# Six loops of a one-core transformer kernel written out as straight code, and a reordered state space layer

## The reference

```python
x = x + L0_xattn(layernorm(x), ctx, ctx, mask)   # 16 heads, softmax over 257 context rows
x = x + L0_attn(layernorm(x))                    # state space layer: s_t = A_t*s_(t-1) + Bx_t, 16 states per channel
x = x + L0_ffn(layernorm(x))                     # 256 -> 1024 -> 256 with quantized hidden values
x = x + L1_xattn(layernorm(x), ctx, ctx)         # 16 heads, sigmoid scores
x = x + L1_attn(layernorm(x))                    # self attention, softmax over 32 tokens
x = x + L1_ffn(layernorm(x))                     # 8 experts, each token goes to the likeliest
```

## Time and profile before

| | us |
|---|---|
| median of 3 runs | 3127.29 (3118.89 to 3130.5) |
| the profiled execution's own time | 3123.87 |
| its span, first to last instruction | 3122.1 |
| `softmax_attention` | 17 to 955 |
| `state_space` | 955 to 1470 |
| `quantized_ffn` | 1470 to 1624 |
| `sigmoid_attention` | 1624 to 2324 |
| `self_attention` | 2324 to 2667 |
| `sort_tokens`, `expert_tiles` | 2667 to 2805, to 3122 |

### The profile page before, as it was taken

How to read it: one execution, slowest core, us unless ns; L and a number is a source line. 1 busy time by engine, 2 the same in 40 slices (tenths; PEclk the granted TensorE clock), 3 DMA queues, 4 the chain that set the end, 5 groups by cost and what they waited for, 6 DMA issues and landing times. The chain is left out here.

```text
span 3122.1 us, 105389 instructions
## 1 busy us (share of the span) xinstructions
PE 2561.8 (82%) x38670; PEld 2034.0 (65%) x38671; DVE 2130.9 (68%) x4719; ACT 1878.5 (60%) x4388; POOL 1542.9 (49%) x1680
## 2 busy tenths in 40 slices
PE   3989889899893899996778989989967878509888
PEld 2867777677782577774446868768755666507666
DVE  5978878788794788886355757657665887643333
ACT  3867667677684788883346767667654665333333
POOL 4655656556562355552006656656635776052222
PEclk9999999999996899998898999999987998559999
DMA  4212212112110000000003212112100000641110
GB/s 144 67 59 59 64 51 64 58 51 64 57 30 14 1 1 1 0 1 14 16 14 91 66 50 62 59 52 61 59 18 3 2 2 2 206 159 34 33 34 27
DMA packets 120602, 144.45 MB, mean 46 GB/s; under 512 B 12912, under 2 KB 111632, under 8 KB 118064
## 3 DMA queue, kind: packets, MB, share of 16 engines
q1 hardware_dynamic: 115568, 124.40, 13.2%
q0 software_dynamic: 4672, 14.57, 1.3%
HBM read 123.71 MB, written 15.22 MB: 44 GB/s over the span
## 5 line engine op out<-in xcount | busy, mean ns | idle before, releaser
L1368 DVE SCALAR_TENSOR_TENSOR x_pTl<-x_psS,x_pTh 128x1024 f16<-128x1024 f32 x128 | 156.8, 1225 | 206.8 <-ACT x_pTh L1276 206.8
L2077 DVE TENSOR_TENSOR_SCAN m_s<-m_a,m_psBx 128x2048 f32<-128x2048 f32 x64 | 282.6, 4415 | 16.0 <-PE m_psBx L1852 15.6
L791 DVE CUSTOM_DVE_ANT_0 x_prob<-x_psS,x_masked,x_prob 128x256 f32<-128x256 f32 x512 | 216.6, 478 | 73.5 <-PE x_psS L548 71.7
L664 ACT ACTIVATE x_prob<-x_prob,x_low 128x257 f32<-128x257 f32 x512 | 253.5, 503 | 20.6 <-DVE x_low L791 20.6
L680 ACT ACTIVATE x_kh<-x_psK,x_bk 128x256 f16<-128x256 f32 x256 | 107.5, 471 | 238.9 <-PE x_psK L432 238.9
L1863 PE MATMUL m_psS<-m_s,all_ident 128*128 128x256 f32 x1024 | 237.3, 385 | 0.9 <-DVE m_s L2077 0.9
L1863 PEld LDWEIGHTS m_psS<-m_s,all_ident 128*128 128x128 f32 x1024 | 190.0, 190 | 46.3 <-issue 21.5
L1984 ACT ACTIVATE m_a<-m_dt,m_rate 128x248 f32<-128x248 f32 x512 | 205.6, 490 | 4.3 <-DVE m_s L2077 4.1
L2982 ACT ACTIVATE e1t_g<-e1t_psH,e1t_bias 128x128 f32<-128x128 f32 x312 | 89.2, 368 | 194.5 <-PE e1t_psH L2931 194.5
L1057 POOL TENSOR_TENSOR x_qbdh<-x_qh,all_mask4h 128x1024 f16<-128x1024 f16 x32 | 60.6, 1895 | 226.7 <-DVE x_ql L1349 226.7
L806 DVE SCALAR_TENSOR_TENSOR x_pTl<-x_psT,x_pTh 128x512 f16<-128x512 f32 x256 | 163.5, 679 | 4.9 <-ACT x_pTh L672 4.0
(11 more groups left out here) (558 smaller groups left out, 10542.0 us busy)
## 6 DMA issues: line engine op xcount, KB each, us to landing
x_ctx<-in_ctxT SPq DMA_DIRECT2D x64, 1024.0 KB, 5.7
x_mraw<-in_mask SPq DMA_DIRECT2D x128, 128.5 KB, 2.7
e1r_stage<-in_L_ffn_w SPq DMA_DIRECT2D x16, 1024.0 KB, 5.0
e_rows<-e1r_pad POOLq DMA_DIRECT2D x1, 5070.0 KB, 19.5
e1t_row<-e_rows SPq DMA_DIRECT2D x39, 130.0 KB, 2.1
all_xres<-in_x SPq DMA_DIRECT2D x1, 4096.0 KB, 14.8
x_vxr<-x_vx SPq DMA_DIRECT2D x128, 32.0 KB, 3.2
x_vxr<-x_vx SPq DMA_DIRECT2D x96, 8.0 KB, 2.0
```

What stands on the lines that cost most here:

```text
L664: act.activation(prob[c % 4][:, h, :], prob[c % 4][:, h, :], ACT.Exp, bias=low[c % 4][:, h:h + 1], scale=-1.0, accum_out=sm[c % 2][:, h:h ...
L791: dve.tensor_tensor_reduce(prob[c % 4][:, h, 0:LAST], psS[:, to:to + LAST], masked[gp][:, j, 0:LAST], -SC, prob[c % 4][:, h, LAST:S2], ALU ...
L1368: dve.scalar_tensor_tensor(pT[c % 4][1][:].rearrange("p r k n -> p (r k n)"), psS[c % 2][:], PS, pT[c % 4][0][:].rearrange("p r k n -> p ( ...
L2077: dve.tensor_tensor_scan(rows(S), rows(A), psBx[:], 0.0, ALU.mult, ALU.add).then_inc(scan_done, 1)
```

## The change

The loops of `softmax_attention`, `sigmoid_attention`, `quantized_ffn`, `state_space`, `self_attention` and `expert_tiles` become straight code on every engine. The loops of `sort_tokens` and of the layer norm's statistics stay. In `state_space` five pieces change places as well. The first hunk of `run` stands six times, at lines 249, 979, 1469, 1667, 2173 and 2878 of before; it is shown once.

```diff
@@ -249,10 +249,8 @@
         def run(eng, body):
-            body(0)
-            with eng.Fori(1, LASTI) as i:
+            for i in range(LASTI + 1):
                 body(i)
-            body(LASTI)
...
@@ -1754,10 +1746,9 @@
                 for c in range(U):
                     if exists(i, c, 1):
                         spread_b(*at(i, c, 1))
+                        dt_u(*at(i, c, 1))
                     if exists(i, c, -2):
                         residual(*at(i, c, -2))
-                    if exists(i, c, 1):
-                        dt_u(*at(i, c, 1))
@@ -1899,14 +1890,14 @@
                     drive(i, c, 2)
                     state_sum(i, c, 0, 0)
+                    if exists(i, c, 2):
+                        dbl(*at(i, c, 2))
                     if exists(i, c, -1):
                         out(*at(i, c, -1))
-                    if exists(i, c, 2):
-                        dbl(*at(i, c, 2))
                     drive(i, c, 3)
-                    state_sum(i, c, 0, 1)
                     if exists(i, c, 2):
                         dt_c(*at(i, c, 2))
+                    state_sum(i, c, 0, 1)
@@ -2000,10 +1991,10 @@
                 for c in range(U):
+                    if exists(i, c, 1):
+                        softplus_log(*at(i, c, 1))
                     decay(i, c, 1, 0)
                     decay(i, c, 1, 1)
-                    if exists(i, c, 1):
-                        softplus_log(*at(i, c, 1))
@@ -2114,9 +2105,9 @@
                     scan(i, c, 2)
                     if exists(i, c, 2):
                         lo_pb(*at(i, c, 2))
-                    scan(i, c, 3)
                     if exists(i, c, -1):
                         gate(*at(i, c, -1))
+                    scan(i, c, 3)
```

## The result

| | median us | runs |
|---|---|---|
| before | 3124.8 | 3118.89 to 3130.5 |
| after | 2881.9 | 2880.12 to 2884.12 |

A forecast was written before the change was run, and what follows sets the result against it. PE was taken as the bound, its gaps in softmax_attention being stalls at the backward branch. Gains of 98 + 45.5 + 25.5 + 4 + 32 = 205 us from 3123.9 gave 2919, predicted as 2920, range 2892 to 2968.

The forecast's parts named there:

- Each iteration becomes like the first, 49.8 us.: softmax_attention: without backward branches every iteration takes as long as the loop's first, which no stall precedes.
- the term of 98: softmax_attention: gain of 98 us from removing 13 backward branches, bounds 71 and 108.
- just this argument for `expert_tiles`: expert_tiles: tiles take 7.06 us straight, 7.64 in the loop, because register instructions stand ahead of matmuls that wait for nothing else.
- The stall itself: softmax_attention: PE alone waits at the jump back, 5.465 us in the median, read as its code being fetched anew.
- 45.5 said: sigmoid_attention: gain of 45.5 us, with six of 13 branches stalling and 38.5 us for an iteration without a stall.
- 25.5 said: expert_tiles: gain of 25.5 us, from 24 tiles at the straight code's 7.06 us; 8 from below.
- 4 said, bounds 0 and 5: self_attention: gain of 4 us, 3.3 from the iteration that begins with a stall, perhaps 1 from the other.
- 32 said: state_space: the reordering takes a step from 26.81 to 24.6 us, 32 us in all, bounds 0 and 39.
- two waits one after the other: state_space: PE's waits per step, 2.0 us for u cured by the Ln's move, 0.75 for the Abs by dt_c's.
- the step of 24.1: state_space: PE's step of 26.81 us less waits of 1.97 and 0.75, giving the gain's upper bound of 39 us.
- The fetch of straight code page after page: Whole kernel: each page of PE's code shows its fetch, some 1.1 us, costing 360 us, so 3280; chance 3%.
- That the state space layer gives nothing: state_space: ACT's fourth table load, or xnT or lo_u as the next wait, removes the gain; 2952 us, chance 13%.

The follow-up runs named there:

- x0_rest_loop: Changed kernel with the softmax_attention loops put back on SP, POOL, ACT and DVE, PE left straight; 2884.58 us.
- x0_reg_addr: Changed kernel, still straight code, but PE computes the last_scores addresses in softmax_attention from a register holding 0; 2915.59 us.
- x0_pe_loop: Changed kernel with the loop of 14 put back in softmax_attention on PE alone; 3005.85 us.
- e1t_carry_ln_back: Changed kernel with the expert's number kept between bodies of expert_tiles and the Ln back behind the decay in state_space; 2878.87 us, ratio 0.9193.
- x0_pe_loop_kx0: Changed kernel with softmax_attention's loop back on PE, but last_scores reading the last key row at a fixed address; 2979.32 us.

## Why the prediction was wrong, step by step

**softmax_attention, the step that failed.** "Each iteration becomes like the first, 49.8 us." The first iteration of the loop is free of a stall but not of register work, so it is a measure of a loop without its branch, not of straight code. I had seen the difference and bounded it by "about 0.7 us" an iteration without a row behind that number. It measured 2.8 from the traces (49.8 to 47.0), of which 0.3 belongs to the loops of the other engines (47.4 in x0_rest_loop), and 2.25 by itself (49.25 to 47.0, x0_reg_addr). So the term of 98 left out 32 to 36 us of register work over the 14 iterations. The row that tells it stands in the trace of before: the same matmuls in the straight code ahead of the loop take a third of the time. And I had made just this argument for `expert_tiles`, and not carried it over. The layer's account: 70.6 us for the 13 stalls of before (their sum), 32.7 for registers, 21.6 for what follows a stall (13 x 1.66), 4.6 for the other engines: 129.5 of 135.3. All but the first are taken from other kernels, two of them with loops whose stalls were not of the same length; 5.8 us are not accounted for.

**The stall itself** was read rightly: only PE has it, it goes with the branch, and a packet of q8 lands 1.3 to 1.5 us before each stall of `softmax_attention` ends. By the rule of the Trainium skill's "Advanced Engine Details and Errata", Control Flow Timing (108 ns), next to nothing could have been won here; x0_pe_loop has 4.6 us for a taken branch, the taken branches of `sigmoid_attention` that do not stall have 0.21 to 0.23, and only the last, not taken, is near the page's price with 0.083. What the Trainium skill's "Runtime: NRT & Kernel Launch", Instruction fetch mechanics, says of a taken branch agrees as far as there is a stall. The two pages held, of which it speaks, do not fit: iterations of some 1720 instructions on PE moved no packet of q8 at all, where a stalled one moves nine of 16 KB. Nor does it tell why the same loop stalls 6 times in one program and 13 in another.

**sigmoid_attention.** 45.5 said, 46.1 measured, by the same method that failed next door. It held because the steps of this layer hardly pay for registers: 38.5 us in the loop and 38.3 in straight code. The forecast was taken from the very trace whose stalls it was to remove. That the count of stalls was 6 is a property of that build, so this number could not have been told from the code.

**expert_tiles.** 25.5 said, 23.6 measured. The tile takes 7.06 as forecast, but each eighth 7.6 to 7.8, for the read at the start of a body, which I had not counted: three such tiles in the 24 make up the 1.9 us that are missing. e1t_carry_ln_back gave 2.7 us back for all four.

**self_attention.** 4 said, bounds 0 and 5; 8.1 measured (8 to 10 by the other runs of the same code, 333.2 to 335.5). The straight code that I compared with was fair: 68.6 us for four steps, and a steady step after is 17.23 (first `psS` matmul to the next step's). But it is 17.3 to 18.4 in each step of the loop, in the iteration without a stall as well, and 18.9 in the step behind the loop: nine steps that take 160.9 us before and 155.1 after, 5.8 less. The other 2.3 us lie outside these steps. No experiment took this apart, and why the steps are slower is open.

**state_space.** 32 said, 27.6 measured: step 24.89 for 24.6. The size was near, partly by luck, and the reason mostly wrong: most of the gain is that of `dt_c` on PE's queue, and none of it needs the Ln. I had subtracted two waits one after the other, each with its own cure, though the first (for u) hangs on the same chain as the second (for the Abs). And they were PEld's waits, 2.72 us together, where PE's own were 1.84: that took the step of 24.1, the upper bound of the gain, below the 24.9 us of work that PE has in a step.

**The rivals.** The fetch of straight code page after page, my slower case, did not come: the periods of 47.0 us are even and PE is busy for 46 of them, with seven or eight packets of q8 in each. The fetch by the other engines did not either; their straight code in `softmax_attention` is 4.6 us faster than their loops. That the state space layer gives nothing was refuted.

**The range.** Its low end, 2892, held with 98 to 108 for the first layer; with 135 there it would have reached down to 2892 - 27 = 2865. The bound was drawn by feeling at the one term that carried half of the sum.

## What to carry to other kernels

To price a loop against straight code, compare the same instructions where the trace has them in both, before the loop and in it; an iteration without a stall still pays for its registers. Register arithmetic costs where it stands among short instructions that wait for nothing else, and there a constant address, or one kept in a register, is worth more than its few instructions look. When two moves are made at one chain, ask which of them starts it: here the one at the head gave most of the gain, and the one at the end gave nothing beside it. And take the waits of the queue that is the bound: a wait of the weight loads is not all time of the matmuls. When an engine's branch stalls, look whether a packet of its instruction queue lands just before the branch ends.

## What the runs showed of the hardware

- The length of the stall at PE's backward branch changes with small edits elsewhere: medians of 5.47 us before, 4.61 in x0_pe_loop, 5.91 in x0_pe_loop_kx0 for nearly the same body; 6 of 13 at 6.7 us and 13 of 13 at 5.1 for the same one. So a time of a kernel with such loops is in part luck of the build.
- A stall there is a wait for code: a 16 KB packet of the instruction queue q8 lands 1.3 to 1.5 us before it ends, in 52 of 52 stalls of four traces. A taken branch without a stall takes 0.21 to 0.25 us, and in `sigmoid_attention` the iteration behind it, some 1720 instructions of PE, moves no packet of q8.
- DVE's backward branch took 0.056 us in the median in the same program.
- The time of before was 3098.7, 3109.7 and 3123.5 us in the three sets of experiments, each on another chip, and in the last its 11 runs went from 3119.5 to 3153.0. The medians of the straight builds that keep the gain stayed within 2879 to 2882 on all three chips, and 12 runs of two of them within 2876.1 to 2882.4. Whether the stalls account for that was not looked into.
- A register-computed address ahead of each three matmuls of two columns nearly triples their time (1.9 for 0.7 us per 24, x0_reg_addr), and PE is recorded as busy meanwhile. The register work elsewhere in the body cost nothing that showed (x0_pe_loop_kx0, first iteration 47.0 us).
